# Layernorm scales computed in another order: variances one tile earlier, roots two weight halves later, ten inputs requested before the loop

## The reference

```python
x = L0_attn_x                        # (4, 512, 512)
xn = _layernorm(x, axis=-1)          # (x - mean) / sqrt(var + 1e-5), per token
x = x + attention(xn) + ffn(xn)
# attention: qk = xn @ Wqk.T + b (8 heads of 8), v = xn @ Wv.T + b, softmax(q k^T) / 8, @ v, @ Wo.T + b
# ffn: logits = xn @ W_gate + b; the top 2 of 8 experts per token
#      y_all = relu(xn @ W_e[e] + b_e[e]);  y = mean of the two chosen rows
```

## Time and profile before

| | |
|---|---|
| Median of 3 runs | 361.82 us (358.92 to 364.0) |
| The profiled execution | 363.15 us, its span 361.4 us |
| Busy share of the span | PE 86%, DVE 64%, POOL 56%, ACT 48% |
| Mean granted TensorE clock | 0.927 of full speed |
| DMA moved | 59.60 MB, mean 165 GB/s |

### The profile page before, as it was taken

One profiled execution on the slowest core, in us unless ns is written; L12 is line 12 of the kernel. 1 busy time (PEld: TensorE's weight loads), 2 busy tenths in 40 slices (PEclk: granted clock), 3 DMA queues, 4 the chain that ended last, 5 costly groups with the idle time before them and its releaser, 6 DMA issues.

```text
span 361.4 us, 5494 instructions
## 1 busy us (share of the span) xinstructions
PE 309.9 (86%) x1629; PEld 222.8 (62%) x1629; DVE 230.7 (64%) x498; ACT 174.2 (48%) x311; POOL 200.9 (56%) x179
## 2 busy tenths in 40 slices
PE   2785976175999999999999899399999999999973
PEld 1574976174888888888888688154546645544421
DVE  4767767871343444766767864967786977884313
ACT  1658775041234333332323243456777677677650
POOL 3366899208686866666565723847388887100000
PEclk9989689555999999999999999769999999999999
DMA  7899975505245445564444511349999999510113
GB/s 206 306 407 378 273 242 166 233 0 170 92 150 172 146 146 176 163 217 147 153 139 150 134 67 60 116 127 172 308 241 183 213 188 142 118 61 0 58 60 117
DMA packets 31004, 59.60 MB, mean 165 GB/s; under 512 B 5504, under 2 KB 5632, under 8 KB 30848
## 3 DMA queue, kind: packets, MB, share of 16 engines
q1 hardware_dynamic: 20864, 39.59, 31.3%
q0 software_dynamic: 7728, 18.62, 25.0%
q10 hardware_dynamic: 2384, 1.04, 1.1%
HBM read 38.52 MB, written 18.61 MB: 158 GB/s over the span
## 4 chain that ended last, share of the span: by engine, by line
PE 83%; issue 6%; DVE 4%; ACT 4%; ACTq 2%; DMA 1%; DVEq 0%; POOLq 0%
PE ps_s L1114 30%; PE ps_t L1051 11%; PE ps_o L1066 9%; PE ps_s L980 8%; PE ps_s L1040 7%; PE ps_t L1094 5%; PE ps_m L1011 3%; PE ps_t L966 2%; PE ps_s L1084 2%; ACT probs L664 2%; PE ps_m L1015 1%; PE ps_o L1040 1%; DMA row_in<-xn_rows,gather_i 1%; PE ps_m L1023 1%; PE ps_m L1024 1%
## 5 line engine op out<-in xcount | busy, mean ns | idle before, releaser
L1114 PE MATMUL ps_s<-w_split,t_hi 128*128 x312 | 101.1, 405 | 2.0 <-issue 2.0
L664 ACT ACTIVATE probs<-ps_t 128x512 f32<-128x512 f32 x128 | 69.7, 597 | 34.6 <-PE ps_t L1051 29.6
L846 DVE TENSOR_REDUCE row_max<-ps_s 128x1 f32<-128x512 f32 x112 | 72.3, 684 | 15.6 <-PE ps_s L1040 10.1
L490 POOL TENSOR_TENSOR row_mid<-row_mid,bias_o 128x512 f32<-128x512 f32 x39 | 50.8, 1302 | 43.8 <-ACT row_mid L611 43.8
L611 ACT ACTIVATE row_mid<-row_mid 128x512 f32<-128x512 f32 x39 | 24.7, 633 | 92.8 <-DVE row_mid L867 80.3
L1114 PEld LDWEIGHTS ps_s<-w_split,t_hi 128*128 128x128 f32 x312 | 56.4, 191 | 13.0 <-issue 2.7
L1114 PE MATMUL ps_s<-w_split,t_lo 128*128 x156 | 61.7, 396 | 0.0
L1051 PE MATMUL ps_t<-q_t,k_head 128*128 128x512 f32 x128 | 57.2, 458 | 3.1 <-ACT probs L664 2.7
L521 POOL DMA_INDIRECT acc<-expert_rows,slots_i x32 | 49.7, 1552 | 16.0 <-issue 8.4
L1051 PEld LDWEIGHTS ps_t<-q_t,k_head 128*128 128x128 f32 x128 | 23.9, 191 | 44.3 <-ACT probs L664 29.7
L471 POOL DMA_INDIRECT row_in<-xn_rows,gather_i x39 | 37.9, 972 | 22.1 <-DVE gather_i L824 15.8
(11 more groups left out here) (133 smaller groups left out, 412.8 us busy)
## 6 DMA issues: line engine op xcount, KB each, us to landing
expert_rows<-row_mid SPq DMA_DIRECT2D x39, 256.0 KB, 2.0
stage<-in_L_ffn_W_e_dram SPq DMA_DIRECT2D x16, 512.0 KB, 7.0
xn_rows<-row_mid SPq DMA_DIRECT2D x16, 256.0 KB, 5.3
acc<-in_L_attn_x_dram SPq DMA_DIRECT2D x16, 256.0 KB, 3.8
out_dram<-res SPq DMA_DIRECT2D x16, 256.0 KB
row_in<-in_L_attn_x_dram SPq DMA_DIRECT2D x8, 256.0 KB, 6.3
w_split<-in_L_attn_x_dram SPq DMA_DIRECT2D x8, 256.0 KB, 8.6
bias_e<-in_L_ffn_b_e_dram SPq DMA_DIRECT2D x1, 2048.0 KB, 7.7
```

The costliest lines, as they stand in the source:

```text
L490: pool.tensor_tensor(row_mid[:, n % 4, :], row_mid[:, n % 4, :], bias_o[:], ALU.add).then_inc(y_done, 1)
L664: act.activation(probs[:, n % 2, j, :], ps_t[:, j % 2, :], ACT.Exp).then_inc(exp_done, 1)
L846: dve.tensor_reduce(row_max[:, b % 2, h, i:i + 1], score_bank(n), AX.X, ALU.max).then_inc(max_done, 1)
L1114: mm = pe.matmul(ps_s[:, n % 2, :], a[:, n % 2, ks], rhs, start=(k == 0), stop=(k == 3 * KC - 1))
```

## The change

Three things move; no instruction is added or removed.

1. VectorE's look-ahead is seven tiles in place of six from step 1 on (step 0 takes tiles 5, 6 and 7). `variance(2)`, `variance(3)` and `variance(4)` so stand in steps 0, 4 and 8, one step earlier. `scales(2)` to `scales(4)` stay in steps 1, 5 and 9, but stand right behind `low(i)`, ahead of that step's `moments`, `keep_proj` and `top`.
2. GpSimd makes the roots of groups 2, 3 and 4 ahead of weight halves 2, 6 and 10 (counted from 0), in place of 1, 4 and 8.
3. SyncE requests ten input tiles ahead of its loop in place of eight; in the loop it requests tile i + 10 where it requested tile i + 8.

```diff
--- before.py
+++ after.py
@@ -34,7 +34,8 @@
 RS = 3
 GROUPS = ((0, 2), (2, 4), (4, 8), (8, 12), (12, 16))
 RX = 14
-ROOT_AT = {1: 2, 4: 3, 8: 4}
+XF = 10
+ROOT_AT = {2: 2, 6: 3, 10: 4}
 K_LAY, Q_LAY = (0, 2, 3, 0), (0, 1, 2, 3)
 
 
@@ -345,13 +346,14 @@
             load_w(0)
             load_x(RI)
             load_w(1)
-            load_x(RI + 1)
+            for i in range(RI + 1, XF):
+                load_x(i)
             for i in range(NT):
 
                 sp.wait_ge(xn_made, i + 1)
                 sp.dma_start(xn_dram[i * P:(i + 1) * P, :], row_mid[:, i % 4, :]).then_inc(xn_out[i % 4], 16)
-                if i + RI + 2 < NT:
-                    load_x(i + RI + 2)
+                if i + XF < NT:
+                    load_x(i + XF)
                 if i + 2 < NT:
                     load_w(i + 2)
 
@@ -751,10 +753,11 @@
                               ALU.subtract).then_inc(weights_split, 1)
             scales(1)
             moments(4)
-            ahead = {0: (5, 6), 1: (7,)}
             for i in range(NT):
                 low(i)
-                for k in ahead.get(i, (i + 6,)):
+                if i in (1, 5, 9):
+                    scales(i // 4 + 2)
+                for k in (5, 6, 7) if i == 0 else (i + 7,):
                     if k < NT:
                         moments(k)
                         if k % 4 == 3:
@@ -763,9 +766,6 @@
                     keep_proj(i - 1)
                 if i >= 1:
                     top(i - 1)
-                for k in ahead.get(i, (i + 6,)):
-                    if k < NT and k % 4 == 3:
-                        scales(k // 4 + 1)
                 if i == 4:
                     dve.wait_ge(weights_split, 5)
                     dve.tensor_tensor(wo_lo[:], ps_s[:, 2, :], wo_hi[:].bitcast(F32), ALU.subtract).then_inc(weights_split, 1)
```

## The result

The changed kernel takes 370.27 us (median of 4 runs, 367.43 to 371.44) against 360.37 us (median of 4 runs of the kernel before, taken with it). The ratio is 1.0258 with a 95% interval of 1.0194 to 1.0322: slower by 2.6%, 9.9 us in the medians, where 8.6 us were forecast. The changed kernel taken once more (e9) gives 1.0228 (1.0148 to 1.0308), 8.0 us in the medians. The changed kernel's profiled execution took 369.46 us, its span is 367.7 us.

The account below looks back on a forecast made before the run. TensorE's matmuls bound the whole span, but in the first 61 us TensorE pauses where VectorE waits for roots. Delays of 3.3 + 3.0 + 2.3 = 8.6 us on 361.82 gave 370.4 us, 8-in-10 range 366.3 to 374.3.

Parts of the forecast that it names:

- the one named: On GpSimd, late roots stand behind low parts of weight halves, so VectorE idles 4 us before scales(2), (3) and (4).
- the second half of the step: On VectorE, scales 0.75, moments 0.82, keep_proj and top 0.73 us stand between the root and low(2) or low(6).
- the sum: Stage one: delays of low(2), low(6) and low(10) add up, 3.3 + 3.0 + 2.3 = 8.6 us.
- The clock: TensorE in stage one: as many projections at the lower clock as before, so nothing was added for it.
- rival 2: Behind each longer TensorE pause one more projection runs at 1.2 GHz: 4.6 us on top, 375.0 us; chance 0.16.
- the second term: Group 3: late root and work behind its scales make low(6) start 3.0 us later, at 38.03 where it was 34.99.
- The wait for group 2: VectorE ahead of scales(2): idle 4 us until GpSimd's root ends at 21.92, scales starting at 22.03.
- The end of the stage: Stage one ends with the last keep_proj, which starts near 69 us; the delays sum to 8.6 us.
- The slots: Behind stage one: slots last as before; GpSimd's 15.77 us idle ahead of the first gather covers its 8.6 us delay.
- Rival 1: GpSimd's roots are done in time, VectorE's waits and at most 5.64 us of TensorE pauses go: 356.2 us; chance 0.05.
- Rival 3: One projection less at 1.2 GHz behind each pause, or delay partly absorbed: 4.0 us slower, 365.8 us; chance 0.13.
- Rival 4: Early input requests delay weight half 0, sliding the chain under group 2 by up to 1.3 us: 371.7 us; chance 0.03.

Follow-up runs that it names:

- e9: Changed kernel itself, unchanged, run once more as a control and for a second profile; 370.66 us, ratio 1.0228 to the kernel before.
- e1: Changed kernel with the roots back ahead of weight halves 1, 4 and 8, all else kept; 361.11 us, ratio 0.9984 to the kernel before.
- e7: Changed kernel with the scales back at the end of steps 1, 5 and 9, roots still late; 365.8 us, ratio 1.0099 to the kernel before.
- e10: Kernel before, unchanged, run again as a control and for a second profile; 362.33 us, ratio 0.9958.
- e8: Changed kernel with 18 extra unused matmuls ahead of each of projections 2, 6 and 10; 369.05 us, ratio 1.0172 to the kernel before.
- e3: Kernel before with ten input tiles requested ahead of the loop and nothing else; 363.19 us, ratio 1.0052.
- e5: Kernel before with cast and pick written to PSUM and read there, and the mask made by a reduction; 359.84 us, ratio 0.993.
- e11: Kernel before with GpSimd's low parts of the last two weight halves cut to 8 of 512 columns; 359.66 us, ratio 0.991.
- e4: Changed kernel with roots and scales in their old places, leaving seven tiles ahead and ten inputs; 360.4 us, ratio 0.9976 to the kernel before.
- e6: Seven tiles ahead, ten inputs, old roots and scales, plus cast and pick through PSUM; 358.93 us, ratio 0.9928 to the kernel before.

## Why the prediction was right, and where it was not

**Cause and sum.** The cause is the one named: e1, which differs from the changed kernel in the roots' places alone, has none of the loss. e7 shows that the second half of the step, what stands behind the scales, was rightly in the sum. How much later than before each point came, in us:

| | low(2) | low(6) | low(10) | last keep_proj |
|---|---|---|---|---|
| forecast | 3.3 | 6.3 | 8.6 | 8.6 |
| changed, against the profile that the prediction reads | 3.1 | 6.2 | 8.5 | 9.5 |
| changed, against e10 | 3.2 | 7.8 | 11.3 | 11.7 |
| changed, second profile (e9), against e10 | 3.7 | 8.4 | 10.8 | 10.3 |
| e8 (pauses filled), against e10 | 3.4 | 6.5 | 9.0 | 8.7 |

Against the profile that it reads, the terms came out as worked out: low(2) was put at 24.33 and started at 24.19, low(6) at 38.03 + 3.3 = 41.3 and started at 41.18, low(10) at 47.38 + 8.6 = 56.0 and started at 55.87. In that profile low(6) and low(10) came 1.6 and 2.8 us later than in e10, though, while e3, e5, e10 and e11 agree on them within 0.6 us. Part of the agreement is therefore luck.

**The clock** is the term that was put too low. The sum "takes as many projections at the lower level as before", and rival 2 held that the pauses of before were enough already to bring the clock down. Behind the first of them that was so only in the profile that was read, where projection 2 took 2.75 us; in e3, e5, e10 and e11 it took 1.56, and in the changed kernel 2.85. From the start of projection 2 to that of wo_hi, which waits for the transposes behind it, are 2.0 us in e10 (21.82 to 23.85) and 3.75 in the changed kernel (24.96 to 28.71). These 1.7 us are what the second term has above its 3.0: low(6) fell back by 4.7 us behind low(2) in both profiles of the changed kernel, and by 3.1 in e8, where projection 2 ran at the upper level. The 16 projections, each from its first matmul to the end of its last, add up to 31.8 us in the profile that was read, 28.9 in e10, 34.9 and 31.5 in the changed kernel and 30.2 in e8. So the waits alone are worth about the 8.6 us of the sum (8.7 in e8), and the clock 1.5 to 3.0 us more, from one or two profiles of each kernel.

**The wait for group 2** was expected at 4 us and is 2.46, though its end is as forecast. The prediction put nothing down for tile 7's moments in their new place. They stand ahead of low(1) now and waited 1.56 us for the input, so low(1) started at 18.73 in place of 16.91 and VectorE came late to a root that was later still. Half 2 landed 1.3 us later, as worked out (22.36 against 21.09), and was hidden.

**The end of the stage** came at 69.70, 0.9 us behind the 68.8 that the sum gives. Between low(10) and the last keep_proj lay 13.83 us where it had been 12.79, but e9 has 12.94 and e10 13.45. That stretch differs by 0.7 and 0.9 us between two profiles of one kernel, so no term of the change can be read from it.

**The slots** were said to last as before. They did not: 17.0 and 17.2 us from the last keep_proj to gather_i in place of 19.6 and 19.0. The step "GpSimd's last low part had 15.77 us of idle time ahead of the first gather, so it does not reach the end of the slots" failed, for the kernel before already, and with it "each microsecond by which stage one ends later or earlier is one of the kernel": in e1 and e4 stage one ends 2.4 and 2.2 us ahead of e10's, and the time is as before. VectorE's cast and pick waited for GpSimd's running split (e5, e11), 3.77 us for both in the profile that was read and 3.13 in e10, where e11 takes 0.62. In the changed kernel GpSimd's splits end at 71.82 and only the cast meets the last of them, 1.13 us for both. So 1.8 to 2.6 us of the loss were given back. gather_i comes 8.5 and 9.7 us later than in e10, which agrees with the 8.0 and 9.9 us of the medians. That this is near the 8.6 of the sum is in part luck too: what the clock added and what the slots gave back nearly cancel.

**The rivals.** Rival 1 (root in time) is out: e1 shows what it would have looked like, and even then the time was not under 360 us. Rival 2 (the clock takes more) was partly true in stage one, as above, but its 375.0 us did not come. Its price was also read too high: the 1.33 us at the upper level is only the part of a projection that lies on the chain, and the whole takes 1.57, so three more at the lower level cost 3.9 us, not 4.6. Rival 3 (less, or part absorbed) was not seen in stage one; what came back, came back in the slots, which no rival named. Rival 4 (early requests) was not seen: half 0 was split at 14.39 against 14.63 on ScalarE. With 2.3 to 2.6% the loss is over 2%, by a margin as thin as the prediction said: both intervals reach below 1.02.

## What to carry to other kernels

A small operation that another engine waits for is as late as the queue of large ones it stands in: count what is ahead of it in its own engine's order, not how early its input is ready. Where a wait can't be avoided, put independent work ahead of it; three pieces of work behind it instead made the same late roots cost 2.3 to 2.6% in place of 1.0. When stage one gets faster and the time does not, compare the length of each operation, not only its idle time. And take a second profile before adding up delays: here the one that was read had a projection at the lower clock that four others had at the upper one, and the extra cost of the change lay just there.

## What the runs showed of the hardware

A VectorE operation can spend its wait for GpSimd as busy time. The cast of 128x32 took 0.19 us with GpSimd idle (e11) and 0.63 to 3.84 beside its splits; pick took 0.43 and 2.50; token_f 0.23 and 1.91. Each long one ended within 0.3 us of the end of a GpSimd split of 2.34 us, mostly of the one then running; e4's cast of 3.84 us passed one such end (58.74) and came through at the next (61.08), and why is open. Operations with an operand in PSUM (low, keep_proj) and the moments of one SBUF tile kept their lengths (0.66 to 0.69, 0.33 to 0.37, 0.68 to 0.69 us) beside the same splits. So did the MAX of top (0.17 us) and in e6 the reduction to `ecol` (0.29), both from SBUF to SBUF, so operands in SBUF alone do not make an operation wait. The Trainium skill (SBUF — State Buffer, section "Terms") calls the port pair that both engines share lock-allocated and held for the full instruction, with the loser fully blocked. The traces agree in that an operation comes through as a split ends, and e5 shows the wait met by a later operation; e4's cast, longer than one split, shows that it need not be the first split to end.

Requests of the same size on SyncE's queue do not take the same time: three took 4.42 us (1.47 each) in the changed kernel, where its first six took 2.81 (0.47 each). The long ones came when nine requests had gone out ahead of them on that queue; what lengthens them was not tested.
